# Eight linear-attention layers and an expert layer on one core: the last layer's first pair moved one slot ahead, two pairs routed inside the last slots, and the experts' token groups cut as three and one

## The reference

```python
def layer(h, p):
    q = phi((h @ wq + bq).reshape(b, s, 16, 8))      # phi = elu + 1
    k = phi((h @ wk + bk).reshape(b, s, 16, 8))
    v = (h @ wv + bv).reshape(b, s, 16, 8)
    kv = einsum('bshd,bshm->bhdm', k, v)
    z = 1.0 / (einsum('bshd,bhd->bsh', q, k.sum(axis=1)) + 1e-06)
    att = einsum('bshd,bhdm,bsh->bshm', q, kv, z).reshape(b, s, d)
    h = ln(h + att @ wo + bo, g1, be1)
    y = gelu(h @ w1 + c1) @ w2 + c2
    return ln(h + y, g2, be2)
...
x = x + final_ln(stack_of_8_layers(layernorm(x)))
xn = ln(layernorm(x), gamma, beta)
w, idx = top_k(softmax(xn @ router_w.T / 1.5), 2)
out = x + layernorm(x) + sum over the two experts of w * (silu(xn @ W1[e]) @ W2[e])
```

## Time and profile before

| | us |
|---|---|
| median of 3 runs (lowest, highest) | 1108.31 (1108.13, 1109.04) |
| profiled execution, own time | 1106.82 |
| its span | 1105.1 |
| TensorE busy in the span | 1013.6 (92%) |
| VectorE busy | 764.8 (69%) |
| ScalarE busy | 836.1 (76%) |
| POOL busy | 797.6 (72%) |

### The profile page before, as it was taken

The page is one execution under the profiler, slowest core; times in us unless marked ns, Lnnn a source line. Parts: engine busy times, 40 slices in busy tenths (PEclk is TensorE's granted clock), DMA queues, the critical chain, the costliest instruction groups (busy, mean ns, idle before and its releaser), DMA issues.

```text
span 1105.1 us, 25020 instructions
## 1 busy us (share of the span) xinstructions
PE 1013.6 (92%) x7766; PEld 953.6 (86%) x7766; DVE 764.8 (69%) x2706; ACT 836.1 (76%) x1621; POOL 797.6 (72%) x1207
## 2 busy tenths in 40 slices
PE   5899899999999999999999999999998648897993
PEld 4798899999999999999999999999998648897992
DVE  6767577777777777777777777777789876443124
ACT  6777688888888888888888888888887637464572
POOL 5958867677767767776777677766777777777772
PEclk9999899999999999999999999999999859999997
DMA  4100010080008003500530080007002145754685
GB/s 135 49 1 16 20 49 1 15 153 24 1 18 165 11 4 66 115 10 15 98 81 1 15 147 31 1 16 150 11 1 59 57 136 178 198 160 144 210 243 170
DMA packets 85154, 82.24 MB, mean 74 GB/s; under 512 B 6779, under 2 KB 65791, under 8 KB 85024
## 3 DMA queue, kind: packets, MB, share of 16 engines
q1 hardware_dynamic: 80480, 72.18, 26.6%
q0 software_dynamic: 4544, 8.47, 2.2%
HBM read 45.15 MB, written 29.44 MB: 67 GB/s over the span
## 4 chain that ended last, share of the span: by engine, by line
PE 71%; DVE 8%; POOL 7%; issue 5%; ACT 4%; DMA 2%; SPq 2%; POOLq 0%; ACTq 0%; DVEq 0%
PE ps L1669 17%; PE ps L1557 8%; PE ps L1559 8%; PE ps L1558 8%; PE ps L1609 7%; PE ps L1603 6%; PE ps L1635 5%; PE ps L1834 4%; PE ps L1817 4%; PE ps L1591 2%; ACT s L895 2%; POOL xs L786 2%; DVE x_lo L1157 2%; DVE stat L1077 1%; DVE mv L1081 1%
## 5 line engine op out<-in xcount | busy, mean ns | idle before, releaser
L1669 PE MATMUL ps<-this_w,hid 128*128 128x128 f32 x2048 | 246.2, 276 | 0.0
L895 ACT ACTIVATE s<-s,shift,rstd 128x128 f32<-128x128 f32 x512 | 210.3, 485 | 45.1 <-POOL shift L606 44.1
L1669 PEld LDWEIGHTS ps<-this_w,hid 128*128 128x128 f32 x2048 | 237.9, 193 | 0.3 <-issue 0.2
L878 ACT ACTIVATE hid<-ps,col 128x512 f32<-128x512 f32 x256 | 155.4, 684 | 3.5 <-PE ps L1559 3.3
L604 POOL TENSOR_TENSOR rstd<-var,neg_half 128x4 f32<-128x4 f32 x136 | 148.6, 1093 | 11.3
L643 POOL TENSOR_TENSOR res_a<-s,row 128x512 f32<-128x512 f32 x60 | 76.8, 1280 | 73.0 <-ACT s L895 73.0
L1557 PE MATMUL ps<-x_hi,this_w 128*128 128x512 f32 x256 | 109.5, 428 | 3.1 <-DVE x_lo L1157 3.1
L601 POOL TENSOR_SCALAR shift<-mv 128x4 f32<-128x4 f32 x136 | 27.5, 202 | 115.2 <-DVE mv L1081 115.1
L1077 DVE BATCH_NORM_STATS2 stat<-s 128x6 f32<-128x128 f32 x512 | 110.1, 276 | 0.0
L1559 PE MATMUL ps<-x_hi,this_w 128*128 128x512 f32 x256 | 101.6, 397 | 0.0
L1558 PE MATMUL ps<-x_lo,this_w 128*128 128x512 f32 x256 | 101.3, 396 | 0.0
(11 more groups left out here) (217 smaller groups left out, 2726.6 us busy)
## 6 DMA issues: line engine op xcount, KB each, us to landing
xs<-pad SPq DMA_DIRECT2D x6, 2925.0 KB, 18.7
res_a<-w SPq DMA_DIRECT2D x39, 256.0 KB
xblk<-xs SPq DMA_DIRECT2D x78, 65.0 KB
raw_w<-w SPq DMA_DIRECT2D x18, 256.0 KB, 7.7
row<-rows SPq DMA_DIRECT2D x9, 512.0 KB, 4.8
this_w<-next_w SPq DMA_DIRECT2D x8, 512.0 KB, 3.2
this_qkv<-next_qkv SPq DMA_DIRECT2D x7, 384.0 KB, 2.6
scaled_w<-w SPq DMA_DIRECT2D x10, 256.0 KB
```

What stands on the lines that cost most here:

```text
L878: a.activation(hid[h][:, c, :], ps(3 + h + c), ACT.Gelu, bias=col[:, bass.ds(lw * FF + (C_C1 + c), 1)]).then_inc(hid_done, 1)
L895: ins = a.activation(dst[:, t, :], src[:, t, :], ACT.Identity, bias=shift[i][:, t:t + 1], scale=rstd[i][:, t:t + 1])
L1669: ins = t_.matmul(ps(3 if h == 0 else 6)[:, t * P:(t + 1) * P], hid[h][:, c, t * P:(t + 1) * P], this_w2[:, c, :], start=c == 0, stop=c == ...
```

## The change

**Order of items.** A list `ORDER` of 32 (layer, pair) takes the place of the slot numbers, and its items 27 and 28 are exchanged: layer 7 of pair 0 stands ahead of layer 6 of pair 3. Functions of `ORDER` say which weights, rows and semaphore counts an item needs. Since two layers' weights are then in use in turns, the last layer reads `next_qkv` and `next_w1`, where they are made, and has its own `last_wo` and `last_w2`. Pair 0 of layer 7 and pair 3 of layer 6 have their inputs transposed in the slot just before their own.

**Routing.** Pair 0 is routed inside slots 30 and 31, all of it. Pair 1 is routed right behind. For pairs 2 and 3 the pieces are spread anew over the blocks, with moments of both halves in one piece, and the inverse roots (`stack_inv`, `sum_inv`, `keep_inv`, and `last_inv` for the last norm of pairs 2 and 3) are now made by VectorE, by an estimate and three Newton steps. The scatters of pairs 2 and 3 are each 16 in a row behind the sends of block 10 and block 29.

**Groups.** The pairs open 9, 16, 30 and 23 blocks: blocks 0, 9, 25 and 55 are the first that need pairs 0, 1, 2 and 3. Six halves' results are loaded between the last blocks, and two at the end.

```diff
-GROUPS = ((0, 1), (2, 3))
+GROUPS = ((0, 1, 2), (3,))
...
+THIRD, THIRDS = 10, 16
+FOURTH, FOURTHS = 29, 16
...
+ORDER = [(l, p) for l in range(LAYERS) for p in range(SLOTS)]
+SWAP = (LAYERS - 1) * SLOTS - 1
+ORDER[SWAP], ORDER[SWAP + 1] = ORDER[SWAP + 1], ORDER[SWAP]
...
+def input_upto(l, s, h):
+
+    l, p = ORDER[l * SLOTS + s]
+    return flips_upto(ORDER.index((l - 1, p)), h) if l else 2 * p + h + 1
...
-                wait(pe, xt_lo_done, upto(l, s, h))
+                wait(pe, xt_lo_done, input_upto(l, s, h))
...
+            def rsqrt(y, v):
+
+                n = v.shape[1]
+                link(d.tensor_scalar(y.bitcast(I32), v.bitcast(I32), -0.5, RSQRT_START, ALU.mult, ALU.add))
+                for _ in range(3):
+                    link(d.scalar_tensor_tensor(out=newton[:, 0:n], in0=v, scalar=-0.5, in1=y, op0=ALU.mult, op1=ALU.mult))
+                    link(d.tensor_tensor(newton[:, 0:n], newton[:, 0:n], y, ALU.mult))
+                    link(d.scalar_tensor_tensor(out=y, in0=newton[:, 0:n], scalar=1.5, in1=y, op0=ALU.add, op1=ALU.mult))
+
+            def last_inv(s):
+
+                dve.wait_ge(mv2_done, upto(LAST, s, 1, base=8))
+                for h in two:
+                    d.tensor_scalar(g_neg[s][:, h * T:h * T + T], mv[2 + h][:, :, 0], -1.0, None, ALU.mult)
+                    ins = d.tensor_scalar(g_one[s][:, h * T:h * T + T], mv[2 + h][:, :, 1], EPS, None, ALU.add)
+                link(ins)
+                rsqrt(g_std[s][:, :], g_one[s][:, :])
+                d.tensor_tensor(g_shift[s][:, :], g_neg[s][:, :], g_std[s][:, :], ALU.mult).then_inc(rstd2_done, 2)
+
+            def stack_inv(p):
+
+                dve.wait_ge(mv0_done, 2 * p + 2)
+                link(d.tensor_scalar(f_var[p][:, :], f_mv[0][p][:, :, 1], EPS, None, ALU.add))
+                rsqrt(f_std[p][:, :], f_var[p][:, :])
...
             for b in range(N_BLOCKS):
                 block_result(b)
-                if b in (1, 2):
-                    outer_residual(b + 3)
-                elif b in (3, 4):
-                    sum_moments(b + 1)
+                if b == 0:
+                    stack_moments(4)
+                    stack_moments(5)
+                elif b == 1:
+                    stack_inv(2)
+                elif b in (2, 3):
+                    outer_residual(2 + b)
+                elif b == 4:
+                    sum_moments(4)
+                    sum_moments(5)
+                elif b == 5:
+                    sum_inv(2)
...
+                elif b == 12:
+                    last_inv(3)
+                elif b == 13:
                     table(2)
...
+                elif b == 17:
+                    stack_moments(6)
+                    stack_moments(7)
+                elif b == 18:
+                    stack_inv(3)
+                elif b in (19, 20):
+                    outer_residual(b - 13)
+                elif b == 21:
+                    sum_moments(6)
+                    sum_moments(7)
+                elif b == 22:
+                    sum_inv(3)
+                elif b == 25:
                     logits(3)
...
             block_features(0)
             block_features(1)
+            last_norm2(2, 0)
+            last_norm2(2, 1)
             for b in range(N_BLOCKS):
                 silu(b)
```

645 lines of the change are left out of this document (344 added, 301 removed).

## The result

| | before | after |
|---|---|---|
| median of 5 runs (lowest, highest), us | 1108.13 (1106.53, 1109.04) | 1097.11 (1092.81, 1099.8) |
| profiled execution: own time, span, us | 1106.82, 1105.1 | 1099.48, 1097.7 |

The ratio is 0.9895, with a 95% interval from 0.9867 to 0.9923. The kernel is 11 us faster; 18 were forecast. Note how the two columns scatter: before spans 2.5 us, after 7. One execution of all that follow, the second of g22, took 1865.84 us at a granted clock of 0.761 and is no part of g22's ratio.

What follows compares the result with a forecast made beforehand. The expert stage was taken to be set by when a pair is routed and scattered, and by VectorE's routing between block results. Block 77 14.2 us earlier plus 4.0 at the end made 18.2, so 1090 us, range 1079 to 1101.

Steps and rivals of the forecast that it cites:

- Term 1: Last slot (31), with pair 0's outer residuals in front: last pair's residual at 857.0, first scatter at 864.1 against 869.64.
- Term 2: First scatter to block 0's result: first flip at 891.3, result about 904 against 906.47, 2.5 us of 6.1 left.
- Terms 3 and 4: Blocks 0 to 25: VectorE takes 16.0 us from 0 to 6, TensorE some 12; block 6 at 920.0, 25 at 965.5.
- Term 4: Blocks 6 to 25: block 25 at 965.5 against 970.86, its 4.85 us wait gone, pair 2's tokens 2 us to spare.
- rival C: VectorE is worse: dearer steps, three more collisions, pair 2's tokens late; 9 us in all, 1099; chance 0.17.
- Term 5: Blocks 25 to 34: nine at 1.89 us plus router product, rank and table loads, 22.0 us; 987.5 against 993.82.
- Term 6: Blocks 34 to 77: pair 3's 5.29 us wait goes, result-load contention 3.6 us (between 2 and 5); 1072.4 against 1086.57.
- Term 7: The end: eight last result loads become four, 4.0 us gained; issues alone give 2.7, full scaling 7.
- B: Block stage: VectorE's new work is hidden and the early start kept; 26 us gained, 1082; chance 0.17.
- D: Blocks: VectorE's stretches idle TensorE, the lower clock costs up to 1.9 us a block; 1116 at 14 blocks; chance 0.04.
- E: POOL's messages: VectorE's operations slow them, 0.3 us longer each gives about 1112; chance 0.02.
- F: Whole kernel: the change doesn't do what it says, the earlier routing is given back wholly, 1108; chance 0.04.

Runs made afterwards that it cites:

- g22: The changed kernel with the groups of the kernel before, (0, 1) and (2, 3), and result loads on the input loads' semaphores: 1093.96 us, ratio 0.9871.
- after_again: The changed kernel run and profiled once more with no edit: 1094.77 us, ratio 0.9898 to the kernel before.
- fine3: ent8 with pair 3's routing cut into smaller pieces over more blocks, no operation added or left out: 1101.86 us, ratio 0.9947.
- ent8: The changed kernel with SyncE reading the table's entries eight at a time instead of four: 1095.09 us, ratio 0.9890.
- g22_ent8: The changed kernel with both edits, groups (0, 1) and (2, 3) and table entries read eight at a time: 1098.15 us, ratio 0.9913.
- before_g31: The kernel before with only the groups changed, to three pairs and one: 1099.49 us, ratio 0.9932.
- norm_late: The changed kernel with pair 2's last norm behind ScalarE's first SiLU and VectorE's last residuals of pair 2 behind block 0's result: 1095.1 us, ratio 0.9895.

## Why the prediction was right, and where its sum was not

**Direction and mechanism.** Faster by earlier routing, with VectorE's new work as what holds the early start back ahead of block 0, and again in 17 to 22: both stand. That the total came inside the range is in part luck, since errors of 3.8 us one way and up to 4.0 the other stand in single terms. The sum was 7 us too large by the median (11 instead of 18), 5.0 us by the profile of after_again (270.2 against 265.2), 12.5 by that of after. The row of after_again minus that of the forecast gives it by terms: +2.0, -0.3, -3.8, +4.0, +0.3, +1.9, +0.9.

**The swap.** Forecast 0.5 us, measured 0.9 ahead of slot 31, with the routing that now stands in slot 30.

**Term 1** was right to 0.1 us in the trace as it stands (residual 857.00, first scatter 863.96 against 864.1). That hides something: slot 31 began at 820.0, 1.65 us before that of before, by the chance of the first 150 us. Counted from slot 31 the residual was 1.65 late; in after_again the first scatter is 43.0 us behind slot 31 (865.09 less 822.07), where the forecast had 42.45. The three collisions that were forecast came, 1.07 to 1.31 us each instead of 0.23.

**Term 2** is where the size of the early start was lost. Scatters and first flip came as forecast (first flip 70.0 us behind slot 31 in after_again, forecast 69.65, before 75.7). ScalarE's norm was what held the first down product, as forecast:
```profile
897.47 3.19 ACT L971 ACTIVATE s<-s,g_shift,g_std 128x128 f32<-128x128 f32 x8 [3.16 <-DVE g_shift L1338]
900.68 1.28 ACT L1077 ACT_TABLE_LOAD   x1
```
But VectorE got there later: pair 1's choices and places met POOL's four residual operations from 886.41 four times, not twice (1.97, 1.29, 0.83 and 0.80 us; the first two alone are 2.8 us above 0.23 each, where I had 1.7 for all). I had 2.5 of the 6.1 us left at block 0; nothing to 0.4 is left. The Trainium skill, "SBUF — State Buffer", section "Who interferes with whom", has a VectorE instruction with two SBUF inputs and a GpSimd instruction that reads SBUF shut each other out. The trace agrees, and shows more: the hit of 1.97 us is longer than one POOL operation there (1.28), so the "up to a whole POOL operation" that I drew from the rule was no upper bound.

**Terms 3 and 4** (0 to 6, 6 to 22). 15.7 us where 16.0 was forecast. The number is right, and the reading "where TensorE needs some 12" beside it is not: TensorE is busy for the whole 15.7 us, and the kernel before took 15.5 with VectorE busy for 9.1 of them. The two engines are about level there. From 6 to 22 I took 40.8 and it was 37.0: 6 to 13 took 16.0 us instead of 19.1 and 16 to 22 took 14.9 instead of 16.0, so part of VectorE's work fits beside TensorE's; which part was not traced. In 17 to 22 VectorE does bound the blocks, as fine3 shows (13.0 us, and 9.5 in smaller pieces). The 3.8 us too many helped the time and harmed the next step.

**Term 4, block 25's tokens, and what stands behind them: the step that failed.** It read "TensorE is there at 960: 2 us to spare". TensorE was there at 955.9 in after (958.30 less 2.43), 957.5 on a scale with slot 31 at 821.65, the tokens at 958.3, on the same scale 959.95, because scatters began at 936.0 rather than 933.7. So 2 us to spare were 2.4 short: rival C's mechanism, which I had given 0.17. That wait alone cost little: ent8 still has it (2.38 us) and takes 26.9 us in 22 to 34, and g22_ent8, without it, 26.2. What cost the time was in no term. A second wait follows, of 2.15 and 3.24 us, for block 27's tokens, behind SyncE's 3.4 us stop; ent8 shows that the stop is its cause. And the lower clock is granted near these waits, for 3.4 us in after_again, 14 in after and none in ent8. In after_again the second wait and half of 3.4 us are 3.9 of the 4.0 us over the forecast; in after the longer wait and half of 14 us come to 10 of its 9.7. With up to 5 us that differ ahead of slot 31 this is enough for the 7 us between after's times; which of the two made them can't be told from one profile.

Term 5 (25 to 34) was forecast at 22.0 us and takes 20.4 in ent8 as in after_again; 22 to 25 was forecast at 4.7 and takes 6.6 in ent8. That ent8 has 26.9 us where the forecast has 26.7 is two errors that cancel.

**Term 6.** The wait for pair 3's tokens went, and 34 to 61 is 51.2 as forecast. The price beside it was too low: 16 blocks of 1.89 are 30.2, so with six halves 61 to 77 is 5.6 to 6.2 us above that, beyond the upper bound of 5; with four it is 1.9 to 2.6. It is the same in before_g31 (36.3) and g22 (32.2), whatever the routing. Not all of it is the loads: ahead of the first, results 61 to 70 take 17.7 us where nine blocks of 1.89 are 17.0, and in after and after_again a clock of 0.69 and 0.67 for five microseconds follows the wait for block 73's tokens.

**Term 7.** 4.0 was forecast, 2.6 and 3.1 measured, next to the lower bound, which counted the issues alone.

**Rivals.** B fell by norm_late: an earlier first product can be had, and it is gone by result 6. D, blocks at the low clock while VectorE works, did not occur: 1.00 from 915 to 955. Its ground, that the lower level is seen only after waits of 4.85 us and more, fell: it came with waits of 2.42 us (after_again) and 1.56 us (g22). The sign "a granted clock under 0.9 from block 1 to 34" was not met as a mean, 0.92 in after and 0.97 in after_again, though 14 us of after stand at 0.50. E did not occur either: pair 0's steps behind the root take 1.25 to 1.45 us, 1.29 on average, where 0.3 more each was its condition. F holds in part: at results 0, 6, 22 and 34 after's profile stands within 1.2 us of before's (905.29, 921.01, 957.76 and 994.20).

**Left open.** Whether the time in 6 to 22 of single profiles (36.6 to 38.7 without the smaller pieces, most of the difference ahead of result 13) is chance or edit; what decides in which wait, and for how long, the lower clock comes; whether earlier messages of pair 2 help. The swap alone wasn't tried, nor the rest without it, so what the swap itself is worth isn't known. The version to keep is g22, the changed kernel with the old groups, at least equal to the change (0.9871 against 0.9895, intervals that overlap) and with one wait less.
